# A byte mask moved from VectorE to ScalarE, and five engines' orders rewritten

## The reference

```python
x = L0_attn_x                                             # 4 x 256 x 256
x = _layernorm(x + L0_attn(x, Wq, Wk, Wv, Wo))            # 32 query heads, 8 key heads, 8 wide
x = _layernorm(x + L0_ffn(x, gate_w, up_w, down_w, scales))
x = _layernorm(x + L1_attn(x, wq, wk, wv, wo))            # 16 query heads, 8 key heads, 16 wide
x = _layernorm(x + L1_ffn(x, lut, gate_idx, up_idx, down_idx))

# L0_ffn: every weight matrix is rounded to an 8 bit float before its matmul
wq = w.astype(jnp.float8_e4m3fn).astype(x.dtype)
# L1_ffn: every weight is taken out of a table of 16 by its index
w = lut[idx]
```

## Time and profile before

| what | us |
|---|---|
| three timed runs | 336.48, 337.21, 332.85; median 336.48 |
| the profiled execution | 333.81, of it span 331.6 |
| TensorE busy | 300.7 (91% of the span) |
| VectorE busy | 255.1 (77%) |
| ScalarE busy | 234.9 (71%) |
| GpSimd busy | 199.4 (60%) |
| mean granted TensorE clock | 0.943 of full speed |

### The profile page before, as it was taken

How to read it: one execution, slowest core, us unless ns; L and a number is a source line. 1 busy time by engine, 2 the same in 40 slices (tenths; PEclk the granted TensorE clock), 3 DMA queues, 4 the chain that set the end, 5 groups by cost and what they waited for, 6 DMA issues and landing times.

```text
span 331.6 us, 7198 instructions
## 1 busy us (share of the span) xinstructions
PE 300.7 (91%) x2608; PEld 208.8 (63%) x2608; DVE 255.1 (77%) x472; ACT 234.9 (71%) x432; POOL 199.4 (60%) x273
## 2 busy tenths in 40 slices
PE   8555877879899999999999999999999999999993
PEld 7331333324444557678666776877879778879992
DVE  7699998999999999999985987577666744535253
ACT  2768689999997768776967966886685656564340
POOL 5876443562448489696887675655564322847664
PEclk9895768599799999999999999999999999999997
DMA  4563442153302054100320050364041000000001
GB/s 134 142 190 116 130 123 74 54 140 86 112 6 65 19 138 125 36 29 3 82 65 5 16 144 14 107 191 148 3 107 38 2 1 4 32 3 32 2 2 63
DMA packets 24889, 23.07 MB, mean 70 GB/s; under 512 B 3558, under 2 KB 24854, under 8 KB 24854
## 3 DMA queue, kind: packets, MB, share of 16 engines
q1 hardware_dynamic: 24854, 22.61, 23.7%
HBM read 10.47 MB, written 3.26 MB: 41 GB/s over the span
## 4 chain that ended last, share of the span: by engine, by line
PE 69%; DVE 20%; issue 5%; POOL 3%; ACT 1%; POOLq 0%; DVEq 0%; ACTq 0%
PE FB L1301 17%; PE PV L1244 12%; PE MM L1188 9%; PE FB L1330 8%; DVE MX L988 8%; DVE LV L1104 6%; PE SC L1223 4%; PE FB L1273 4%; PE SC L1218 4%; PE FB L1140 3%; PE FB L1256 2%; POOL LV L753 2%; PE FB L1282 2%; DVE QS L941 1%; PE MM L1320 1%
## 5 line engine op out<-in xcount | busy, mean ns | idle before, releaser
L869 ACT ACTIVATE PB<-SC 128x1024 f32<-128x1024 f32 x96 | 98.0, 1021 | 27.8 <-PE SC L1218 14.6
L988 DVE TENSOR_REDUCE MX<-MM 128x2 f32<-128x512 f32 x128 | 81.0, 681 | 4.8 <-PE MM L1188 3.9
L1188 PE MATMUL MM<-KS,QS 62*128 62x256 bf16 (+1 forms) x384 | 58.9, 287 | 15.0 <-DVE MX L988 11.9
L992 DVE TENSOR_REDUCE MX<-MM 128x4 f32<-128x1024 f32 x32 | 39.1, 1221 | 21.9 <-PE MM L1188 21.9
L1244 PE MATMUL PV<-PB,VP 128*32 128x256 f32 x768 | 52.8, 401 | 0.0
L735 POOL TENSOR_TENSOR HL<-HF,HH 128x256 fp32r<-128x256 f32 (+1 forms) x48 | 36.5, 771 | 24.6 <-ACT HH L846 24.5
L1188 PEld LDWEIGHTS MM<-KS,QS 62*128 62x128 bf16 (+1 forms) x384 | 24.4, 97 | 42.6 <-DVE MX L988 28.1
L1104 DVE COPY_PREDICATED LV<-LB,LV 128x1728 f32<-128x1728 uint8 (+2 forms) x30 | 41.2, 1373 | 3.5 <-POOL LV L753 3.1
L1301 PE MATMUL FB<-XH,W 128*128 128x256 f32 x192 | 43.0, 305 | 0.0
L753 POOL TENSOR_SCALAR LV<-LB,LD,LT 128x432 f32<-128x432 uint8 x56 | 38.8, 706 | 1.6 <-DVE LB L1088 0.7
L1301 PE MATMUL FB<-XL,W 128*128 128x256 f32 x192 | 38.5, 282 | 0.0
(11 more groups left out here) (108 smaller groups left out, 597.4 us busy)
## 6 DMA issues: line engine op xcount, KB each, us to landing
QS<-QP SPq DMA_DIRECT2D x48, 128.0 KB, 2.4
IX<-in_idx SPq DMA_DIRECT2D x10, 216.0 KB, 3.3
dw<-LO SPq DMA_DIRECT2D x10, 216.0 KB, 2.2
W1L<-dw SPq DMA_DIRECT2D x10, 216.0 KB, 2.8
KS<-KP SPq DMA_DIRECT2D x24, 64.0 KB, 2.0
XT<-in_xt SPq DMA_DIRECT2D x4, 256.0 KB, 3.1
X<-in_x SPq DMA_DIRECT2D x4, 256.0 KB, 3.0
KS<-KP SPq DMA_DIRECT2D x24, 32.0 KB, 1.9
```

The costliest lines, as they stand in the source:

```text
L869: act.activation(PB[:, quad % PB_QUADS, kt, :, :], SC[:, :, :], ACT.Exp, scale=DH[layer(j)] ** -0.5).then_inc(exp_done, 1)
L988: dve.tensor_reduce(mx[:, f, :], MM[:, 2 * f:2 * f + 2, :], axis=AX.X, op=ALU.max).then_inc(max_red, 1)
L992: dve.tensor_reduce(mx, MM[:, :, :].rearrange("p (f i) s -> p f i s", f=2), axis=AX.X, op=ALU.max).then_inc(max_red, 2)
L1188: ins = pe.matmul(MM[:, 2 * f + i, :], QS[lo:lo + r, j % NST, qs + h, qt * P:(qt + 1) * P], keys(j)[lo:lo + r, j % NST, ks, :], start=True ...
```

## The change

The mask is no longer made on VectorE. ScalarE takes the absolute value of `Q8B` times a quarter and writes it as bytes, which are not zero for the large weights; VectorE's copy takes these bytes as its mask as before. ScalarE's step has five activations instead of four. The semaphore `big_done` and both waits for it go. ScalarE waits, for chunks after the first, for VectorE's copy of the previous chunk (`q8_used`), since that copy reads `BIG`; VectorE waits only for `q8_cast`, which comes with the last of the five activations.

All five order strings are written anew. They hold the same steps: of TensorE's 540 steps 252 stand at another place, of ScalarE's 343 170, of VectorE's 246 62, of GpSimd's 171 57, of SyncE's 123 109. Most move by one to three places. The diff, with the orders cut to lines of the first jobs:

```diff
     "PE": (
-        "q.0.0@1 q.0.1 kv.0.0@2 kv.0.1 kv.1.0@0 q.1.0@1 q.1.1 kv.1.1 max.0.0 max.0.1 max.0.2 max.0.3 max.0.4 max.0.5 "
-        "max.0.6 q.2.0@2 max.0.7 kv.2.0@1 mt.0.0@0 max.0.8 q.2.1 max.0.9 max.0.10 score.0.0 max.0.11 q.3.0@0 max.0.12 "
-        "score.0.1 score.0.2 pv.0.0.0 pv.0.0.1 pv.0.0.2 score.0.3 max.0.13 kv.2.1 max.0.14 score.0.4 max.0.15 score.0.5 "
-        "max.1.0 mt.0.1@1 max.1.1 score.0.6 max.1.2 pv.0.0.3 score.0.7 pv.0.1.0 pv.0.1.1 score.0.8 max.1.3 pv.0.1.2 "
-        "pv.0.1.3 score.0.9 max.1.4 score.0.10 kv.3.0@1 max.1.5 score.0.11 max.1.6 pv.0.2.0 max.1.7 score.0.12 max.1.8 "
...
+        "q.0.0@1 q.0.1 kv.0.0@2 kv.0.1 q.1.0@1 q.1.1 kv.1.0@0 kv.1.1 max.0.0 max.0.1 max.0.2 max.0.3 max.0.4 max.0.5 "
+        "max.0.6 q.2.0@2 max.0.7 kv.2.0@1 mt.0.0@0 max.0.8 q.2.1 max.0.9 max.0.10 max.0.11 score.0.0 kv.2.1 score.0.1 "
+        "q.3.0@0 score.0.2 pv.0.0.0 pv.0.0.1 max.0.12 score.0.3 max.0.13 max.0.14 max.0.15 score.0.4 max.1.0 score.0.5 "
+        "max.1.1 score.0.6 mt.0.1@1 max.1.2 pv.0.0.2 score.0.7 pv.0.0.3 pv.0.1.0 kv.3.0@1 score.0.8 pv.0.1.1 pv.0.1.2 "
+        "max.1.3 score.0.9 pv.0.1.3 score.0.10 max.1.4 kv.3.1 max.1.5 score.0.11 pv.0.2.0 max.1.6 max.1.7 score.0.12 "
...
     "ACT": (
-        "lutix.0 q.0 kv.0 qmid.0 kmid.0 lut1.0.2 lut1.0.3 lutix.1 q8.0 lutlow.0 q.1 q8.1 lutix.2 qmid.1 kv.1 lut1.1.2 "
-        "lut1.1.3 q8.2 q8.3 kmid.1 q8.4 lutlow.1 mt.0.0 q8.5 lut1.2.2 lut1.2.3 score.0.0 q.2 score.0.1 lutix.3 "
-        "score.0.2 q8.6 score.0.3 lutlow.2 kv.2 score.0.4 q8.7 score.0.5 lut1.3.2 lut1.3.3 mt.0.1 score.0.6 q8.8 "
-        "score.0.7 qmid.2 lutix.4 score.0.8 lutlow.3 score.0.9 kmid.2 stage.0.0 score.0.10 lut1.4.2 score.0.11 q8.9 "
-        "score.0.12 lut1.4.3 score.0.13 mt.1.0 lutix.5 score.0.14 q8.10 score.0.15 lutlow.4 score.1.0 stage.0.1 kv.3 "
-        "score.1.1 lut1.5.2 score.1.2 lut1.5.3 score.1.3 back.0.0 back.0.1 q.3 score.1.4 q8.11 score.1.5 wo.0 mt.1.1 "
...
+        "lutix.0 q.0 kv.0 qmid.0 lutix.1 lut1.0.2 lut1.0.3 kmid.0 q8.0 q.1 lutlow.0 q8.1 qmid.1 lut1.1.2 lut1.1.3 q8.2 "
+        "q8.3 lutix.2 kv.1 q8.4 kmid.1 lutlow.1 mt.0.0 q8.5 lutix.3 lut1.2.2 lut1.2.3 score.0.0 q.2 score.0.1 kv.2 "
+        "score.0.2 q8.6 lutlow.2 score.0.3 q8.7 score.0.4 lut1.3.2 score.0.5 lut1.3.3 score.0.6 mt.0.1 q8.8 score.0.7 "
+        "qmid.2 lutix.4 score.0.8 lutlow.3 score.0.9 kmid.2 stage.0.0 score.0.10 lut1.4.2 score.0.11 q8.9 score.0.12 "
+        "lut1.4.3 score.0.13 mt.1.0 lutix.5 score.0.14 q8.10 score.0.15 lutlow.4 score.1.0 kv.3 stage.0.1 score.1.1 "
+        "lut1.5.2 score.1.2 lut1.5.3 back.0.0 score.1.3 back.0.1 q.3 score.1.4 q8.11 score.1.5 wo.0 mt.1.1 score.1.6 "
...
     "DVE": (
-        "lutbits.0 scales lut2.0 lut3.0 lut4.0 q8.0 lutbits.1 max.0.0 max.0.1 max.0.2 max.0.3 q8.1 max.0.4 lut2.1 q8.2 "
-        "max.0.5 lut3.1 max.0.6 q8.3 max.0.7 lut4.1 mt.0.0 q8.4 lutbits.2 max.0.8 max.0.9 max.0.10 max.0.11 lut2.2 "
-        "lut3.2 q8.5 max.0.12 lut4.2 max.0.13 q8.6 max.0.14 max.0.15 lutbits.3 mt.0.1 q8.7 max.1.0 max.1.1 max.1.2 "
-        "lut2.3 lut3.3 lut4.3 max.1.3 max.1.4 lutbits.4 q8.8 max.1.5 max.1.6 max.1.7 max.1.8 mt.1.0 q8.9 max.1.9 lut2.4 "
...
+        "scales lutbits.0 lut2.0 lut3.0 lut4.0 q8.0 lutbits.1 max.0.0 max.0.1 max.0.2 max.0.3 q8.1 max.0.4 lut2.1 q8.2 "
+        "max.0.5 lut3.1 q8.3 max.0.6 lut4.1 max.0.7 mt.0.0 q8.4 lutbits.2 max.0.8 max.0.9 max.0.10 max.0.11 lut2.2 "
+        "lut3.2 lut4.2 q8.5 max.0.12 max.0.13 q8.6 max.0.14 max.0.15 lutbits.3 mt.0.1 q8.7 max.1.0 max.1.1 lut2.3 "
+        "lut3.3 lut4.3 max.1.2 lutbits.4 q8.8 max.1.3 max.1.4 max.1.5 max.1.6 max.1.7 mt.1.0 q8.9 max.1.8 lut2.4 lut3.4 "
...
     "POOL": (
-        "ones.0 ones.4 qdif.0 kdif.0 lut1.0.0 lut1.0.1 q.0 kv.0 q8w.0 lutlow.0 qdif.1 lut1.1.0 q.1 lut1.1.1 q8w.1 q8w.2 "
-        "kdif.1 kv.1 q8w.3 q8w.4 lutlow.1 lut1.2.0 lut1.2.1 q8w.5 q8w.6 kdif.2 lutlow.2 q8w.7 qdif.2 lut1.3.0 lut1.3.1 "
-        "lutlow.3 q8w.8 lut1.4.0 lut1.4.1 q.2 kv.2 q8w.9 lutlow.4 lut1.5.0 lut1.5.1 q8w.10 qdif.3 kdif.3 xadd.0 wo.0 "
...
+        "ones.0 ones.4 qdif.0 kdif.0 lut1.0.0 lut1.0.1 q.0 kv.0 lutlow.0 q8w.0 qdif.1 lut1.1.0 lut1.1.1 q8w.1 q8w.2 "
+        "q8w.3 kdif.1 q.1 q8w.4 lutlow.1 kv.1 lut1.2.0 lut1.2.1 q8w.5 kdif.2 q8w.6 qdif.2 lutlow.2 q8w.7 lut1.3.0 "
+        "lut1.3.1 lutlow.3 q.2 q8w.8 lut1.4.0 lut1.4.1 kv.2 q8w.9 q8w.10 lutlow.4 kdif.3 lut1.5.0 lut1.5.1 xadd.0 "
+        "qdif.3 wo.0 q8w.11 lutlow.5 xd.0 lut1.6.0 lut1.6.1 lut1.6.2 lut1.6.3 q.3 hsplit.0.0 lutlow.6 lut1.7.0 kv.3 "
...
     "SP": (
-        "load.0 ldix.0 ldix.1 qstack.0.0 ldxt.1 ldxt.2 kstack.0.1 ldq8.0 ldq8.1 kstack.0.0 qstack.0.2 qstack.0.1 "
-        "kstack.0.2 ldxt.3 ldix.2 ldix.3 ldq8.2 kstack.1.0 ldq8.3 qstack.1.0 lutlow.0 qstack.1.2 ldq8.4 ldx.0 ldx.1 "
-        "ldq8.5 mt.0.0 qstack.1.1 lutlow.1 ldix.4 kstack.1.2 kstack.1.1 ldq8.6 ldq8.7 ldix.5 ldq8.8 ldq8.9 mt.0.1 "
-        "lutlow.2 lutlow.3 qstack.2.0 ldix.6 ldq8.10 qstack.2.1 kstack.2.0 kstack.2.2 mt.1.0 kstack.2.1 load.1 ldix.7 "
-        "lutlow.4 qstack.2.2 kstack.3.0 ldq8.11 mt.1.1 lutlow.5 qstack.3.0 kstack.3.1 mt.2.0 ones.4 qstack.3.2 ldx.2 "
...
+        "load.0 ldix.0 ldix.1 ldq8.0 qstack.0.0 ldxt.1 ldq8.1 kstack.0.0 ldix.2 ldxt.2 qstack.0.1 qstack.0.2 kstack.0.1 "
+        "kstack.0.2 qstack.1.0 ldxt.3 ldq8.2 ldix.3 lutlow.0 ldq8.3 ldq8.4 ldq8.5 qstack.1.1 kstack.1.0 ldq8.6 mt.0.0 "
+        "ldix.4 kstack.1.2 qstack.1.2 kstack.1.1 ldq8.7 lutlow.1 lutlow.2 ldix.5 ldq8.8 mt.0.1 ldq8.9 qstack.2.0 "
+        "kstack.2.0 kstack.2.1 qstack.2.2 ldq8.10 mt.1.0 kstack.2.2 load.1 lutlow.3 lutlow.4 qstack.2.1 ldix.6 ldq8.11 "
+        "ldx.0 qstack.3.0 mt.1.1 lutlow.5 load.2 ldix.7 kstack.3.1 mt.2.0 qstack.3.1 qstack.3.2 ldx.1 ones.4 lutlow.6 "
...
@@ -420,7 +420,6 @@
         down_half = sem("down_half")
         th_done = sem("th_done")
         q8_cast = sem("q8_cast")
-        big_done = sem("big_done")
         x_sum = sem("x_sum")
         lut_steps = sem("lut_steps")
         q8_used = sem("q8_used")
@@ -889,12 +888,13 @@
                     act.wait_ge(ld_raw[c % 2], 16 * (c // 2 + 1))
                     if c >= 1:
                         act.wait_ge(q8_cast, c)
-                        act.wait_ge(big_done, c)
                     act.activation(Q8A, RAW[:, c % 2, :], ACT.Copy, saturate=False)
                     act.activation(Q8B, RAW[:, c % 2, :], ACT.Copy, scale=0.25, saturate=False).then_inc(q8_bytes, 1)
                     act.wait_ge(q8_bytes, c + 1)
                     if c >= 1:
                         act.wait_ge(q8_done, c)
+                        act.wait_ge(q8_used, c)
+                    act.activation(BIG[:, :], Q8B, ACT.Abs, scale=0.25)
                     act.activation(QA, Q8A, ACT.Copy)
                     act.activation(QB, Q8B, ACT.Copy, scale=4.0).then_inc(q8_cast, 1)
                 elif kind == "lutix":
@@ -1070,12 +1070,6 @@
                 elif kind == "q8":
 
                     c = step[1]
-                    dve.wait_ge(q8_bytes, c + 1)
-                    if c >= 1:
-                        dve.wait_ge(q8_used, c)
-                    dve.tensor_scalar(BIG[:, :].bitcast(I32), Q8B.bitcast(I32), 0x40404040, None,
-                                      ALU.bitwise_and).then_inc(big_done, 1)
-                    dve.wait_ge(big_done, c + 1)
                     dve.wait_ge(q8_cast, c + 1)
                     dve.copy_predicated(QA, BIG[:, :], QB).then_inc(q8_used, 1)
                 elif kind == "lutbits":
```

## The result

The changed kernel takes 338.51 us in the median of 20 runs (335.07 to 340.82), the kernel before 335.29 in 20 runs beside them (331.62 to 337.21). The ratio is 1.0114 with a 95% interval of [1.008, 1.0148]: 1.1% slower, 3.8 us [2.7, 5.0]. The forecast was no change, 335.0 us; the time lies inside its range (329.5 to 340.3), but the kernel did move, to the side that the forecast had not taken. The profiled execution took 337.74 us with a span of 335.5 (333.81 and 331.6 before). Runs more than 1.5% above the fastest of the same kernel are left out of the ratios and of the counts by clock further down, one of the changed kernel, four of the kernel before beside the experiments, two each of e1, e6 and h1 and one of f1; all but one of them (380.54 us) stand close to the others, at low granted clocks.

The account below looks back on a forecast made before the run. VectorE was taken to pace the first third, TensorE the part from 130 us. Terms −1.9 (eight masks), +1.5 (a late maximum), +0.5 (60 to 100 us), −0.2 (last mask) gave −0.1: 335.0 us, range 329.5 to 340.3.

Parts of the forecast that it names:

- `max.0.12`: Thirteenth maximum of the first batch, moved later in TensorE's order: VectorE waits 2.6 to 2.7 us near 50 us, taken as +1.5.
- the price of the orders: Reordered instruction lists of all engines: +1.5 us, all from one late maximum in the first batch, other moves counted as nothing.
- The other moves: nothing: Other reorderings on TensorE, ScalarE, VectorE and GpSimd in the first third swap neighbours of one batch: 0 us.
- covered: SyncE's later weight load and residual load still arrive before their users need them, the residual by ten microseconds: no cost.
- after 130 us moves are free: Behind 130 us reorderings cost nothing as long as TensorE finds its inputs; that part keeps its length.
- The bounds of ±1 us: Limits on the first third's other reorderings, from VectorE's other waits: 4.7 us of gaps less 1.3 us.
- 60 to 100 us, I take +0.5: ScalarE nearly full there with four chunks' added activations; VectorE's gain will not show; between −0.7 and +1.7 us, taken +0.5.
- The terms of the mask alone: Moving the mask, without orders: −1.9 us for eight masks, +0.5 from 60 to 100 us, −0.2 for the last mask.
- none covered: All twelve added ScalarE activations, 0.43 us each, find no gaps to hide in: +5.2 us.
- the full gain: Rival, 0.18: VectorE's whole saving shows, −2.9 us (332.2), or −7.6 (327.5) if its gaps go too; about 330.5 us.
- ScalarE paces: Rival, 0.25: ScalarE sets the first third's pace, added activations uncovered, +1.7 to +5.2 us; about 338.5 us.
- +2.3 us for the move: By the rule preferring VectorE for simple element-wise work: 5.2 us added on ScalarE less 2.9 saved on VectorE.

Follow-up runs that it names:

- e1: The changed kernel (mask on ScalarE) with all five engine orders of the kernel before; 336.21 us, ratio 1.0018 to the kernel before.
- e6: The kernel before with one TensorE step, for the first batch's thirteenth maximum, moved later; 335.96 us, ratio 0.9985.
- h1: The changed kernel's code with the old orders and 27 extra TensorE matmuls that feed nothing; 335.34 us, ratio 0.9963 to the kernel before.
- f1: The changed kernel's code, four computing engines on old orders to about 60 us, then new, SyncE's old throughout; 350.37 us, ratio 1.0451.
- the ladder of lists: Changed kernel's code, new orders added in steps: none +0.6 us, SyncE's +1.5, all engines to 60 us +2.6, to 120 us +3.3, all +3.8.

## Why the prediction was wrong

The engine that paces was read rightly. VectorE's masks were priced at 2.9 us and measured at 2.4 and 2.8; the activation at 0.43 us a step and measured at that; the wait at `max.0.12` came in its place with 1.98 us. The step that failed on every count is the price of the orders: +1.5 in all, with nothing for the moves other than `max.0.12`. How much the mask's own terms add depends on the lists beside them.

*"The other moves: nothing", SyncE's "covered", and "after 130 us moves are free".* All lists together cost 3.2 us with the mask on ScalarE (±1.7), 4.9 with it on VectorE (±1.4) and 5.0 without a mask (±1.8), not 1.5. Between the two profiles 3.15 us are lost ahead of job 3's first exponential and 0.75 behind it, and no step of the ladder of lists is larger than 1.1 us. The bounds of ±1 us had been drawn from VectorE's gaps as they were in one profile. Which moves cost it stays open.

*"`max.0.12`, I take +1.5."* The wait was real, its price was not. Its durations came from the earlier trace rows at the clock that these happened to have; at the same clock the new early lists make VectorE wait 0.4 to 0.7 us more, and the rest of the 1.98 us goes with the clock. Removed, it comes back at the next maximum.

*"60 to 100 us, I take +0.5."* The terms of the mask alone, −1.9 + 0.5 − 0.2 = −1.6 us, measured +0.6 with the old lists, 2.2 us too low, and −1.1 with the new, 0.5 too low and within the noise. With the old lists twelve activations cost 3.0 to 3.4 us, between all covered (0) and none covered (5.2), and beyond the +1.7 that was set as the upper bound for this stretch; with the new, 1.2. The bound counted ScalarE's own time. It left out TensorE's clock, which fell to 0.50 in e1's profile there. In the changed kernel's profile VectorE waits 0.7 us for maxima from 60 to 85 us, where it waited 4.8 in e1's.

So the 3.9 us between −0.1 and +3.8 are 1.7 of the orders and 2.2 of the mask if the mask is moved first, 3.4 and 0.5 if the orders are changed first. One slip in the sums changes nothing: the middle of the full gain, 332.2 and 327.5, is 329.85 and not 329.5.

The rival "ScalarE paces", at 0.25, had 338.5 us, and that is the time that came. It was not the mechanism, and that the time fits is luck: with the old lists the mask on ScalarE is +0.6 us. By the rule from the Trainium skill, page "ScalarE: Activation LUTs", section "Rules for kernel authors", the prediction had worked out +2.3 us for the move; these runs give +0.6 [−0.6, +1.8] with the old lists and −1.1 (±1.8) with the new, so they do not bear it out.

How much of the 3.8 us is the clock? Over all runs, 34 of the kernel before with a mean clock of 0.94 and more have a median of 333.0 us, 41 below 0.926 one of 335.9. Of the changed kernel, 4 runs above have 335.8 and 12 below 339.0. At an equal mean clock it is 2.7 to 3.1 us slower; the rest would be that it reaches 0.94 less often (4 of 19 runs, 34 of 109; below 0.926 are 12 and 41), which at these counts is not clear of chance. Of the 2.7, half a microsecond to 0.75 lies behind job 3's first exponential and the mask's part is between −1.1 and +0.6; the rest could not be pinned to a step.

What was missing is a case in which small waits at TensorE, each worth tenths, change its clock, and with it all durations taken from rows.

## What to carry to other kernels

Read the granted clock beside every TensorE duration before it goes into a sum, and price a wait of TensorE at both levels: here the same order of work made VectorE wait 0 us at 1.00 and 3.4 us at 0.50. Where an engine other than TensorE sets the pace and TensorE's gaps leave it at the lower level, work that feeds nothing can shorten the kernel: 27 matmuls with the old orders gave 1.8 us [0.8, 2.9], the best version here that computes everything; with the new orders 27 and 54 gave nothing that can be measured. And when a change has two halves, cost the half that looks like housekeeping with the same care; here moving the mask did little, and rewriting the orders around it lost the time.
